# A causal attention layer on one core: the probabilities of one query tile in four are turned by VectorE blocks and small transfers instead of TensorE transposes

## The reference, cut to what matters

```python
x: (4, 512, 256)                         # b rows of 512 tokens
xn = layernorm(x)
Q = xn @ Wq + bq; K = xn @ Wk + bk; V = xn @ Wv + bv   # 16 query heads, 4 key heads, 128 wide
scores = Q K^T / sqrt(128) + causal mask
attn = softmax(scores)
ctx = attn @ V
y = gelu(ctx @ Wo + bo)
s = layernorm(xn + y) * gamma + beta
g = silu(ffn(xn))                        # gate/up 1024, down 256
out = x + s * g
```

## Time and profile before

| | us |
|---|---|
| three executions | 726.42, 727.29, 732.52 (median 727.29) |
| profiled execution: span from first to last instruction | 725.2 |
| TensorE busy in the span | 679.8 |
| VectorE, ScalarE, GpSimd busy | 493.0, 428.5, 280.1 |

### The profile page before, as it was taken

One profiled execution on the slowest core, in us unless ns is written; L12 is line 12 of the kernel. 1 busy time (PEld: TensorE's weight loads), 2 busy tenths in 40 slices (PEclk: granted clock), 3 DMA queues, 4 the chain that ended last, 5 costly groups with the idle time before them and its releaser, 6 DMA issues.

```text
span 725.2 us, 13208 instructions
## 1 busy us (share of the span) xinstructions
PE 679.8 (94%) x4032; PEld 594.3 (82%) x4032; DVE 493.0 (68%) x1636; ACT 428.5 (59%) x1011; POOL 280.1 (39%) x328
## 2 busy tenths in 40 slices
PE   2799999999899999999899999999999999999993
PEld 1678888888788888898788888887888898888872
DVE  6955433335777777778668677776777778867777
ACT  2423233326666667677667676866667677767671
POOL 2499100000523324157615142583324157615234
PEclk9699999999999999999999999999999999999998
DMA  8334000002000000000200000002000000200000
GB/s 273 116 117 145 1 29 0 30 0 88 1 1 2 1 1 1 1 1 1 91 2 1 2 1 1 2 4 89 1 1 1 1 1 1 88 1 2 0 1 30
DMA packets 14522, 20.52 MB, mean 28 GB/s; under 512 B 752, under 2 KB 12144, under 8 KB 14192
## 3 DMA queue, kind: packets, MB, share of 16 engines
q1 hardware_dynamic: 13328, 14.37, 6.0%
q0 software_dynamic: 1120, 5.24, 2.2%
HBM read 15.41 MB, written 4.19 MB: 27 GB/s over the span
## 4 chain that ended last, share of the span: by engine, by line
PE 84%; DVE 7%; ACT 3%; issue 3%; DMA 1%; SPq 0%; POOL 0%; DVEq 0%; ACTq 0%
PE bank L941 40%; PE down_ps L941 34%; PE down_ps L1028 8%; PE bank L1015 2%; DVE cT_lo L808 2%; ACT cT_hi L690 2%; DVE hidT_lo L754 1%; DMA raw<-in_wgu 1%; PE bank L994 1%; ACT probs L681 1%; DVE xnT_lo L739 1%; DVE pT_lo L792 1%; DVE xn L731 0%; DVE stats L716 0%; ACT wgu_hi L593 0%
## 5 line engine op out<-in xcount | busy, mean ns | idle before, releaser
L551 POOL TENSOR_TENSOR probs<-probs,inv 128x512 f32<-128x512 f32 (+3 forms) x256 | 181.1, 721 | 390.9 <-DVE inv L892 390.7
L681 ACT ACTIVATE probs<-probs,least 128x512 f32<-128x512 f32 (+3 forms) x256 | 142.4, 558 | 46.5 <-DVE least L885 45.0
L885 DVE CUSTOM_DVE_ANT_0 probs<-bank,mask 128x512 f32<-128x512 f32 (+3 forms) x256 | 121.4, 487 | 11.7 <-issue 11.2
L687 ACT ACTIVATE pT_hi<-down_ps 128x512 fp32r<-128x512 f32 x156 | 92.7, 594 | 49.1 <-PE down_ps L1028 41.8
L792 DVE TENSOR_TENSOR pT_lo<-down_ps,pT_hi 128x512 fp32r<-128x512 f32 x156 | 107.0, 686 | 17.4 <-ACT pT_hi L687 14.3
L1028 PE MATMUL down_ps<-ident,probs 128*128 128x128 f32 x624 | 93.5, 272 | 2.3 <-POOL probs L551 2.3
L1028 PEld LDWEIGHTS down_ps<-ident,probs 128*128 128x128 f32 x624 | 75.4, 140 | 14.8 <-POOL probs L551 2.5
L941 PE MATMUL down_ps<-wo_lo,cT_hi 128*128 128x256 f32 x256 | 73.5, 287 | 4.1 <-DVE cT_lo L808 3.0
L803 DVE SCALAR_TENSOR_TENSOR qT_lo<-bank,bias,qT_hi 128x512 fp32r<-128x512 f32 x64 | 47.7, 749 | 41.2 <-ACT qT_hi L671 41.2
L941 PE MATMUL bank<-kT_lo,qT_hi 128*128 128x512 f32 (+2 forms) x192 | 70.3, 366 | 2.4 <-issue 2.4
L941 PE MATMUL down_ps<-wo_hi,cT_lo 128*128 128x256 f32 x256 | 72.1, 282 | 0.0
(11 more groups left out here) (136 smaller groups left out, 1603.3 us busy)
## 6 DMA issues: line engine op xcount, KB each, us to landing
x_row<-in_x SPq DMA_DIRECT2D x4, 512.0 KB, 6.8
raw<-in_wgu SPq DMA_DIRECT2D x4, 512.0 KB, 6.0
raw<-in_wq POOLq DMA_DIRECT2D x2, 1024.0 KB, 5.2
raw<-in_wo POOLq DMA_DIRECT2D x2, 1024.0 KB, 6.4
g_scratch<-g_out SPq DMA_DIRECT2D x4, 512.0 KB, 2.9
x_b<-in_x SPq DMA_DIRECT2D x4, 512.0 KB, 3.6
g_b<-g_scratch SPq DMA_DIRECT2D x4, 512.0 KB, 4.6
out<-res SPq DMA_DIRECT2D x3, 512.0 KB, 3.5
```

The source lines that it names most:

```text
L551: nc.gpsimd.tensor_tensor(p, p, inv[:, u % UNITS, g:g + 1].to_broadcast([P, (tile_of(u) + 1) * P]), ALU.mult).then_inc(probs_made, 1)
L681: nc.scalar.activation(p, p, ACT.Exp, bias=least[:, u % UNITS, g:g + 1], scale=-1.0, accum_out=total[:, u % UNITS, g:g + 1]).then_inc(exp_ ...
L687: nc.scalar.activation(hi[:], ps, ACT.Copy).then_inc(probsT_hi, 1)
L885: nc.vector.tensor_tensor_reduce(out=probs[t][:, g, :], in0=ps[:, 0:(t + 1) * P], in1=mask[:, (T - 1 - t) * P:], scale=-SCALE, scalar=BIG, ...
```

## The change

In every segment but the last one, tile 1 is not turned on TensorE any more; 15 of 16 segments have this. Its `probs` tile is kept in another layout: 32-column blocks, the four heads side by side within a block. At the place `t2.2` of its order VectorE waits for all four heads of tile 1 from GpSimd and turns the 32x32 blocks of the whole 128x1024 tile in place, in one instruction (L983 of the changed kernel). Then SP issues 16 transfers from `probs` to the new tile `moved`, each 32 partitions x 2 x 128 elements (32 KB), 512 KB in all. ScalarE, at `t1.0` and `t1.1`, waits for all 16 and makes `pT_hi` from `moved`, VectorE makes `pT_lo` from it. Two new waits replace the order that TensorE's transposes gave: at `t1.0` ScalarE waits until `p2.1` has read its buffer (`pT_read`), at `t1.1` until the context of tile 2 is done. The columns of the turned tile are in block order, and `cT` is written back in the order of heads.

```diff
+BLOCK = 32
+BLOCKS = P // BLOCK
+SHUFFLED = 1
+SHUFFLE_AT = "t2.2"
+SHUFFLES = BLOCKS * BLOCKS
...
+        if step == shuffle:
+            yield "x", shuffled
...
-    probs = [sb(f"probs{t}", [P, G, (t + 1) * P]) for t in range(T)]
+    probs = [sb(f"probs{t}", [P, G * (t + 1) * P]) for t in range(T)]
+    moved = sb("moved", [P, SHUFFLED + 1, BLOCKS, G * BLOCK])
...
+        def shuffle(b, kv):
+            n = b * KV + kv
+            sp.wait_ge(blocks_made, n + 1)
+            if n:
+                before = kv - 1 if kv else KV - 1
+                sp.wait_ge(probsT_split, (b - (kv == 0)) * PAIRS + pair_index(before * T + T - 1 - SHUFFLED, SHUFFLED) + 1)
+            for i in range(BLOCKS):
+                for q in range(BLOCKS):
+                    sp.dma_start(moved[q * BLOCK:(q + 1) * BLOCK, :, i], probs_blocks[i * BLOCK:(i + 1) * BLOCK, :, q]
+                                 ).then_inc(moved_in, 16)
...
         for b in range(B):
+            if b:
+                shuffle(b, 0)
+                sp.wait_ge(out_made, 2 * b)
+                sp.dma_start(out_v[b - 1], res[:]).then_inc(out_stored, 16)
+                sp.wait_ge(out_stored, 16 * b)
             sp.dma_start(x_b[:], x_v[b]).then_inc(x_b_in, 16)
             sp.dma_start(g_b[:], g_v[b]).then_inc(g_b_in, 16)
-            if b < B - 1:
-                sp.wait_ge(out_made, 2 * b + 2)
-                sp.dma_start(out_v[b], res[:]).then_inc(out_stored, 16)
-                sp.wait_ge(out_stored, 16 * b + 16)
+            for kv in range(1 if b else 0, KV - 1 if b == B - 1 else KV):
+                shuffle(b, kv)
...
-                    r = pair_index(*step[1:])
-                    act.wait_ge(probsT_done, b * PAIRS + r + 1)
-                    ps, (hi, _) = transposed(step, end)
-                    nc.scalar.activation(hi[:], ps, ACT.Copy).then_inc(probsT_hi, 1)
+                    _, u, j = step
+                    r = pair_index(u, j)
+                    if is_shuffled(u, end):
+                        act.wait_ge(moved_in, (b * KV + kv_of(u) + 1) * SHUFFLES * 16)
+
+                        if j == 0:
+                            act.wait_ge(pT_read, b * KV + kv_of(u) + 1)
+                        else:
+                            act.wait_ge(ctx_done, b * UNITS + u)
+                        nc.scalar.activation(pT[r % 2][0][:], moved_pair(j), ACT.Copy).then_inc(probsT_hi, 1)
+                    else:
+                        act.wait_ge(probsT_done, b * TRANSPOSED + transposes_before(r, end) + 1)
+                        ps, (hi, _) = transposed(step, end)
+                        nc.scalar.activation(hi[:], ps, ACT.Copy).then_inc(probsT_hi, 1)
...
+                if is_shuffled(step[1], end):
+                    hi, lo = pT[r % 2]
+                    nc.vector.tensor_tensor(lo[:], moved_pair(step[2]), f32(hi[:]), ALU.subtract).then_inc(probsT_split, 1)
...
+                elif step[0] == "x":
+                    dve.wait_ge(probs_made, b * SCORES_ALL + (step[1] + 1) * G)
+                    p = probs[SHUFFLED][:]
+                    nc.vector.transpose(p, p).then_inc(blocks_made, 1)
...
             r = pair_index(u, j)
+            if is_shuffled(u, end):
+                return
...
+            elif tile_of(u) == SHUFFLED + 1 and j == tile_of(u) - 1:
+                last.then_inc(pT_read, 1)
```

More of the change, by code:

```diff
@@ L97 @@
 SCORES_ALL = UNITS * G
+TRANSPOSED = KV * (PAIRS_OF_KV - (SHUFFLED + 1))
 RING_BANKS = 4
@@ L167, in highs_done, with transposes_before, is_shuffled @@
     return step[1] * (PROJ_OF_KV - 1) + sum(w != "V" for w in PROJ[:proj_index(step) % PROJ_OF_KV + 1])
+def transposes_before(r, end):
+    kv, i = divmod(r, PAIRS_OF_KV)
+    shuffled = PAIRS_OF_KV - (SHUFFLED + 1) * (SHUFFLED + 2) // 2
+    return kv * TRANSPOSED // KV + (i if end or i < shuffled else i - (SHUFFLED + 1))
+def is_shuffled(u, end):
+    return tile_of(u) == SHUFFLED and not end
 def ring(last=False):
@@ L205, in scalar_steps, with vector_steps @@
             yield steps[i]
-def vector_steps(steps):
+def vector_steps(steps, kv, end):
     steps = list(steps)
+    shuffle = None if end or kv < 0 else next(segment(kv, text=SHUFFLE_AT))
+    shuffled = kv * T + T - 1 - SHUFFLED
     for i in range(len(steps) + 1):
@@ L319, in build, with probs_row, as_blocks, as_heads @@
     y_ps = down_ps[:, 3, 0:D]
+    def probs_row(u, g, end):
+        t = tile_of(u)
+        if is_shuffled(u, end):
+            return probs[t][:].rearrange("p (k g m) -> p k g m", g=G, m=BLOCK)[:, :, g, :]
+        return probs[t][:].rearrange("p (g n) -> p g n", g=G)[:, g, :]
+    def as_blocks(ap, shuffled):
+        return ap.rearrange("p (k m) -> p k m", m=BLOCK) if shuffled else ap
+    def as_heads(ap, shuffled):
+        return ap.rearrange("p (q g m) -> p g q m", q=BLOCKS, g=G) if shuffled else ap
+    def by_heads(ap, shuffled):
+        return ap.rearrange("p (g q m) -> p g q m", q=BLOCKS, g=G) if shuffled else ap
+    def moved_pair(j):
+        return moved[:, j].rearrange("p q n -> p (q n)")
     def transposed(step, end):
@@ L542, in _, with steps @@
         works = {"residual": residual, "root": root, **{f"out{i}": out_piece(i) for i in range(8)}}
-        def steps(b, order, ends=()):
+        def steps(b, order, ends=(), end=False):
             for step in order:
@@ L561, in _ @@
         for kv in range(1, KV):
-            steps(B - 1, segment(kv, last=kv == KV - 1))
+            steps(B - 1, segment(kv, last=kv == KV - 1), end=kv == KV - 1)
         def tile_root_of(t):
@@ L678, in steps @@
                     _, u, g = step
-                    p = probs[tile_of(u)][:, g, :]
+                    p = probs_row(u, g, end)
                     act.wait_ge(masked, b * SCORES_ALL + u * G + g + 1)
@@ L806, in low_part @@
                 dve.wait_ge(ctx_hi, b * UNITS + step[1] + 1)
-                hi, lo = cT
-                nc.vector.tensor_tensor(lo[:], ctx_ps, f32(hi[:]), ALU.subtract).then_inc(ctx_split, 1)
+                blocks = is_shuffled(step[1], end)
+                hi, lo = (by_heads(w, blocks) for w in (f32(cT[0][:]), cT[1][:]))
+                nc.vector.tensor_tensor(lo, as_heads(ctx_ps, blocks), hi, ALU.subtract).then_inc(ctx_split, 1)
         def xn_again(b):
@@ L869, in tile_output, with steps @@
             nc.vector.tensor_tensor(r, r, x_b[:, t, :], ALU.add).then_inc(tile_out_dve, 1)
-        def steps(b, order, ends=(), row_ends=(), end=False):
+        def steps(b, kv, order, ends=(), row_ends=(), end=False):
             of = banks_last if end else banks
-            for step in vector_steps(order):
+            for step in vector_steps(order, kv, end):
                 if step[0] == "masked":
@@ L882, in steps @@
                     dve.wait_ge(scores_done, b * SCORES_ALL + n + 1)
+                    if t == SHUFFLED and g == 0 and kv_of(u):
+                        dve.wait_ge(moved_in, (b * KV + kv_of(u)) * SHUFFLES * 16)
                     nc.vector.memset(total[:, u % UNITS, g:g + 1], 0.0)
                     nc.vector.tensor_tensor_reduce(
-                        out=probs[t][:, g, :], in0=ps[:, 0:(t + 1) * P],
-                        in1=mask[:, (T - 1 - t) * P:], scale=-SCALE, scalar=BIG, op0=ALU.add, op1=ALU.min,
+                        out=probs_row(u, g, end),
+                        in0=as_blocks(ps[:, 0:(t + 1) * P], is_shuffled(u, end)),
+                        in1=as_blocks(mask[:, (T - 1 - t) * P:], is_shuffled(u, end)), scale=-SCALE, scalar=BIG, op0=ALU.add, op1=ALU.min,
                         accum_out=least[:, u % UNITS, g:g + 1]).then_inc(masked, 1)
@@ L919, in low_of @@
             return "low", (step[0], kv, *step[1:])
-        steps(0, segment(-1, text=FIRST))
-        steps(0, segment(-1, text=AHEAD))
-        steps(0, segment(0))
+        steps(0, -1, segment(-1, text=FIRST))
+        steps(0, -1, segment(-1, text=AHEAD))
+        steps(0, 0, segment(0))
         with dve.Fori(0, B - 1) as b:
             for kv in range(1, KV):
-                steps(b, segment(kv), ((low_of(kv + 1, "k"), xn_again),) if kv == KV - 1 else ())
-            steps(b, segment(KV), row_ends=ROW_END_DVE)
+                steps(b, kv, segment(kv), ((low_of(kv + 1, "k"), xn_again),) if kv == KV - 1 else ())
+            steps(b, KV, segment(KV), row_ends=ROW_END_DVE)
         for kv in range(1, KV - 1):
-            steps(B - 1, segment(kv))
-        steps(B - 1, segment(KV - 1, last=True), ((("masked", LAST + T - 1, 0), xn_again),), end=True)
+            steps(B - 1, kv, segment(kv))
+        steps(B - 1, KV - 1, segment(KV - 1, last=True), ((("masked", LAST + T - 1, 0), xn_again),), end=True)
         tile_output(LAST + 1)
```

20 lines of the change are left out of this document (13 added, 7 removed).

## The result

The changed kernel takes 866.62 us (865.93 to 867.12, 4 runs) where the kernel before takes 728.78 (4 runs on that chip): 1.189 times as long, 95% interval 1.185 to 1.194. The forecast was 769 us with a range of 742 to 803. The direction and the place were right, the size was off by a factor of more than three: 138 us in place of 42.

The account below looks back on a forecast made before the run. TensorE was taken to bound attention. Waits of 23.1 us in 15 segments and 8.7 us at row ends, plus 10.2 us of clock, made 42.0 us on the median of 727.29: 769 us, range 742 to 803.

Parts of the forecast that it names:

- What bounds, and where it waits: In attention TensorE sets the pace; it saves 0.88 us a middle segment but stalls 2.4 us at `p1.0`.
- Step 1 and 2: VectorE at `t2.2`: block transpose starts behind the last reciprocal at about 264.7, takes 1.23 us; `t2.2`'s later low part costs nothing.
- Step 3: SP issues 16 transfers one after the other at a pitch of 0.39 us; fifteen pitches make 5.85 us.
- my upper end of 0.56: Highest issue pitch on SP, from 0.51 us and the gap; a rival (prices at upper ends, chance 0.15) made it 807 us.
- Step 4 and 5: Last transfer lands 1.7 us after issue; high part, low part and hand-overs take 1.40 us, then `p1.0` starts.
- The clock: TensorE's clock falls once in each of three first segments of a row, 3.4 us each, 10.2 us.
- a rival for falls in most segments: Clock falls after stalls in half of the other twelve segments, 789 us, or in all, 810; chance 0.18.
- The ends of rows: Smaller slack at kv = 3 and in first segments adds 0.84 and 2.07 us, three segments each, 8.7 us.

Follow-up runs that it names:

- ten and six: Changed kernel with the block transpose behind V, ten of the 16 transfers issued by SP and six by GpSimd: 732.29 us, 1.005 of the kernel before.
- store and loads: Changed kernel with the block transpose behind V, one store to HBM and four loads replacing 16 moves: 724.58 us, 0.994 of the kernel before.
- the two runs without the first segments: Store-and-four-loads and ten-SP-six-GpSimd versions, only for kv = 1 to 3, first segments of rows as in the kernel before: 721.53 and 722.93 us.

## Why the prediction was wrong

**What bounds, and where it waits: right.** TensorE set the pace, the 0.88 us of two groups of transposes is what a middle segment gives back once nothing waits (33.3 to 32.4), and the wait at `p1.0` is where the loss arises, in every one of 15 segments.

**Step 1 and 2: right.** The start behind the reciprocal, 1.23 us, no loss for `t2.2`.

**Step 3: wrong, the largest error.** The pitch was 0.64 us, not 0.39, and outside my upper end of 0.56: 15 x 0.25 = 3.8 us a segment, 56 us in all. I priced the issues by stores of a tile to HBM that each stood alone behind a wait. Standing alone was not the point: the first move of a segment stands alone too and took 0.59. The stores were another kind of issue, of another shape and to HBM, and the kernel before had no move from SBUF to SBUF to price it by. The earlier trace rows had the 0.51 us of the load issued directly behind another, which I put down to what it reads, and the early stage, which I left out, had SP issues as dear as the moves:

```profile
2.32 1.27 SPq L421 DMA_DIRECT2D raw<-in_wgu  x2
16.61 1.21 SPq L421 DMA_DIRECT2D raw<-in_wgu  x2
```

Two loads of weights in 1.27 us, 0.65 from the start of one to the next: with that row as the upper end the price of a segment would have been inside the bounds. The rule of the Trainium skill (DMA: Bandwidth & Descriptors, Issuing engines are not separate DMA queues), that initiating is usually small beside the DMA itself, does not hold for these transfers: an issue takes 0.60 of the 1.87 us from its start to the landing, and 9.6 us of issues stand ahead of the last transfer.

**Step 4 and 5: too short.** Landing 1.9 for 1.7, and 0.6 us left out: `p1.0` waits for `cT_lo` behind `pT_lo`. Together 0.8 us, 12 us in all.

**The clock: the wrong branch.** I gave it three falls and 10 us, and a rival for falls in most segments. It fell at every one of the 15 stalls. Keeping TensorE busy gave 29 us back, so this term was 19 us short. The rival's mechanism was right, its price was not: it put 3.4 us on a fall, as if all of the 6.8 us at the low level were work, and a middle segment lost 1.7 to 1.9, since 3.3 of these 6.8 us lay inside the stall (0.78 over 7.5 us in the window above).

**The ends of rows: the stalls right, the rest missing.** I had 8.7 us for kv = 3 and the first segments. The stalls came as figured: 7.6 us at kv = 3 and 8.5 in the first segments, 0.85 and 1.8 more than the 6.74 of a middle one, where I had 0.84 and 2.07. But measured against a middle segment's own growth of 7.8, kv = 3 grew by 1.9 more (43.0 us) and the first segments by 4.8, 4.9 and 3.2 (49.0, 49.0 and 44.3 against 36.4, 36.3 and 33.3), 18.6 us together, 10 more than I had. Part is the clock's again: with TensorE kept busy the same sum is 14 us. Part stands further on in two of the first segments, where the wait for `pT_lo` at L873 grew from 1.8 to 2.8 us. And part is there without any transfer, where the first segments still grow by 0.6 to 1.5 us when they should shrink by 0.9; the last point below bears on it.

The terms add up to 42 + 56 + 12 + 19 + 10 = 139 us where 138 were measured, but the last two overlap. With the ends taken from the run that kept TensorE busy (5 in place of 10) the sum is 134, and 4 us stay unexplained. My bounds were drawn around the wrong row, so the range missed as well. (One of its sums is off by 1 without bearing on this: 727.3 + 31.8 - 6 is 753, not 752.)

## What to carry to other kernels

Count DMA instructions on the path before bytes: a run of small transfers on one queue costs its number times the pitch of issues that follow each other directly, of the same shape and between the same kinds of memory, and the price of another kind of issue is no bound for that. Five transfers through HBM (2.6 + 3 x 0.65 + 3.0 = 7.6 us from the blocks on) beat sixteen direct ones (11.5). A stall of TensorE has a second price after it, and idle time on TensorE can be tested for that price by filling it with passes that nobody reads. When a consumer is late, read all its waits: the next buffer to be freed may stand one instruction behind the one that you watch.

## What the runs showed of the hardware that was not expected

- With 128 partitions and one run of 64 elements, an issue on SP took 0.34 us alone and 0.43 directly behind another for loads from and stores to HBM, and 0.53 and 0.60 for SBUF to SBUF. From SBUF to SBUF an issue behind another took 0.59 to 0.62 us with 16 to 64 KB and 32 to 128 partitions alike. Not every load from HBM was cheaper: those of `moved` from `spare` took 0.56 and 0.61. GpSimd issued the moves in 0.54 us, ScalarE in 0.62.
- The clock fell to 1.2 GHz at each of the 15 stalls of 6.7 to 8.6 us in the changed kernel and of 3.0 to 5.3 us with the earlier block transpose. With eight transfers twelve of the stalls were of 1.8 to 2.7 us, and it fell at four of these, at one of 1.85 us and not at one of 2.74.
- VectorE's low part with both inputs in SBUF took up to 1.16 us in place of 0.68 where GpSimd was at work on the row's end. In the run without transfers:

```profile
L863 DVE TENSOR_TENSOR pT_lo<-probs,pT_hi x30: 678/681/1158, 209.5 to 675.9; 128x512 fp32r<-128x512 f32 x30
```

```profile
341.98 1.15 DVE L863 TENSOR_TENSOR pT_lo<-probs,pT_hi 128x512 fp32r<-128x512 f32 x1
```

```profile
338.35 5.93 POOL L595 TENSOR_TENSOR res<-res,rowc 128x512 f32<-128x512 f32 x4 [2.12 <-DVE res L910]
```

  With an input in PSUM it took 0.68 at the same place of the kernel before, beside the same work of GpSimd, whose four products there took 5.0 us and now 5.9. It came again at all three row ends of every run in which these low parts met that work (without transfers, eight transfers, the earlier block transpose, ten and six, store and loads), up to 1.82 us, and nowhere in the changed kernel, where they came too late to meet it, nor in the two runs without the first segments. With the store and the loads:

```profile
335.45 1.78 DVE L874 TENSOR_TENSOR pT_lo<-moved,pT_hi 128x512 fp32r<-128x512 f32 x1 [0.16 <-ACT pT_hi L763]
```

  There TensorE waited 1.6 us at `p1.0` in the three first segments and in no middle one, so this is at least part of what they lose, beside the 1.23 us of the block transpose ahead of the row's end; no run separates the two. It agrees with the Trainium skill (SBUF — State Buffer, Who interferes with whom), by which a VectorE operation with two SBUF inputs contends with a GpSimd operation that reads SBUF.
